# Four float32 products of a transformer block's cross stage, each written as three products of rounded parts that share tiles

## The chip, the core and the metric

The kernel runs on one core of a Trainium2 chip, in one launch. Its engines work side by side, each through a list of instructions of its own, and wait for each other by semaphores: TensorE (PE) multiplies, VectorE (DVE), ScalarE (ACT) and GpSimd (POOL) work elementwise, and SyncE (SP) here only issues DMA transfers. The metric is the device time of one execution in microseconds (us), as the median of several runs.

## What is computed

`x` is 16 blocks of 128 rows by 512 columns. Three stages follow each other, each on layer-normalised rows and added back to `x`: attention, the cross stage, and a feed-forward stage (FFN) with quantised weights. In the cross stage a block's 128 rows are the channels and its 512 columns the positions.

```python
def _L0_xattn_ref(mask, encodings, w_in, b_in, w_out, b_out, w_ct, b_ct, local_size):
    ...
    x = jnp.transpose(mask, (0, 2, 1))
    qkv = x @ w_in.T + b_in
    q, k, v = jnp.split(qkv, 3, axis=-1)
    ...
    scores = jnp.einsum('bqhd,bkhd->bhqk', q, k) / jnp.sqrt(jnp.asarray(d, q.dtype))
    ...
    scores = jnp.where(band[None, None], scores, neg)
    attn = jax.nn.softmax(scores, axis=-1)
    o = jnp.einsum('bhqk,bkhd->bqhd', attn, v).reshape(n, t, e)
    o = o @ w_out.T + b_out
    o = jnp.transpose(o, (0, 2, 1))
    y = jax.nn.relu(o) * encodings
    out = jnp.einsum('nit,io->not', y, w_ct) + b_ct[None, :, None]
```

Four of its products have a 128 x 128 weight on one side and a block of 128 x 512 on the other: the queries and the keys (`wqk`, two halves), the heads' output (`wout`), and the product behind the gate (`wct`).

## The kernel before, in words

Attention comes first. It already writes its float32 products as three products of parts: a value is rounded to the type `float32r` (high), the rest is rounded too (low), and high x high, low x high and high x low are summed in PSUM. Its lines 367 to 369 are such a product of 128 x 128 by 128 x 512. A short block of its own (`setup_cross`) then loads the cross stage's weights and makes the row scales; all engines meet at its end.

The cross stage and the FFN are one block (`cross_and_ffn`). It is written as a software pipeline by hand: each engine runs `step(b)` for b = -3 to 15, and in a step works on several blocks at once. A step on PE, ACT and DVE has eight slots (s = 0 to 7). In step b:

- PE, in every slot, first computes a unit of scores of block b+1 whose row maxima are wanted (`maximum_scores`, into PSUM tile `Sm`), then a unit of scores of block b shifted by their maxima (`shifted_scores`, into `Se`). There is one `Sm` and one `Se`: the next unit of `Sm` waits for DVE's maxima of the last one (`mx`, L1583), and the next unit of `Se` for ACT's exponentials (`x_ex`, L1262). Between the units stand the other products: probabilities times values of block b-1 in slots 0 to 2 (L1121), the heads' output of block b-2 in slot 2 (`out_product`, L1131), the values of block b+1 in slot 3 (L1162), the queries and keys of block b+3 in slots 5 and 6 (`project`, L1106), and the product behind the gate of block b-2 in slot 7 (`last_product`, L1139).
- ACT, in slot 2, copies a piece of the FFN's weights (`w_stage`, L1325, in steps 0 to 11); in slot 3 it copies the heads' sums out of PSUM (`x_oU`, L1282), in slot 4 it makes the gate's relu (`gated`, L1287), in slots 4 and 5 a logarithm and two exponentials for 1/sum (`x_rl`, L1291 and L1296), and in slots 6 and 7 the rounded queries and keys (`high`, L1273).
- DVE makes the maxima, the normalised rows of block b+3 (`normalised`, L1567, slot 4), the rests of queries and keys (`rest`, L1573, slots 6 and 7), copies and statistics.
- POOL makes the low parts of maxima, queries and keys (`maxima_low` L1404 and L1406, `low` L1410), multiplies the gate by the context (`gated`, L1415), and scales and merges the heads (`scaled` L1419, `merged` L1424).
- SP sends queries and keys out to DRAM and back into the layout of the scores (tiles `x_Q` and `x_K`), and loads weights' pieces and context.

Every engine works strictly in the order written. The last products of blocks 14 and 15 are written by hand among the first steps of the FFN. PE there has `gate_up(0, 1)`, `last_product(14)`, `rows_turned(1)`, and later `last_product(15)`, `gate_up(1, 2)`, `rows_turned(2)`; ACT has `ffn_step(0)`, `gated(15)`, `ffn_step(1)`. `rows_turned(b)` is the transpose of block b's quantised rows (L1205).

## Time and profile before

| what | value |
|---|---|
| median of the runs (3) | 1137.68 us (1136.1 to 1139.05) |
| the profiled execution's own time | 1140.24 us |
| its span on the core | 1138.4 us |
| busy: PE, DVE, ACT, POOL | 90%, 70%, 58%, 53% |
| cross stage with its fill | about 634 to 972 us of the span |
| mean granted TensorE clock | 0.964 of full speed |

The span is the profiled execution from the first instruction to the last; the difference to its own time (1.84 us) lies around it. The shares of busy time are over the whole span. A matmul record is longer than the time to the next one, since matmuls overlap in the pipeline: what one costs is read from start to start. A float32 product of 128 x 512 shows as two matmul records, one of `float32r` as one.

### The profile page before, as it was taken

The page shows a single profiled execution, that of the slowest core. Times are in us where ns is not written, and L with a number is a line of the kernel's source. Part 1 is how long each engine was busy: PE and PEld are TensorE (multiplying, and loading weights), DVE is VectorE, ACT ScalarE, POOL GpSimd, SP SyncE. Part 2 cuts the span into 40 slices and gives each one's busy share as a digit, 9 for nine tenths or more (in the row PEclk, how much of TensorE's full clock was granted, in tenths as well). Part 3 has the DMA queues.
Part 4 walks back from the last instruction along what each step waited for, and adds up shares of the span by engine and source line. Part 5 has one row for each costly group of instructions (what it writes and reads, how often), then busy time and mean ns, then how long its engine had stood idle before and what let it go on. Part 6 is the DMA issues. An engine that isn't in the chain of part 4 may idle for free. (4 is left out here: it accounts for less than half of the span.)

```text
span 1138.4 us, 25188 instructions
## 1 busy us (share of the span) xinstructions
PE 1025.3 (90%) x9588; PEld 774.2 (68%) x9604; DVE 791.7 (70%) x1444; ACT 665.1 (58%) x1204; POOL 602.7 (53%) x586
## 2 busy tenths in 40 slices
PE   6689999999999999999977378999999998789996
PEld 5578778888888888888855156666666665344443
DVE  6577867666566665666753367787878765699995
ACT  5545555545545454554653236777777666578885
POOL 3564766657567565765663523353535345455552
PEclk9899999999999999999997689999999998899999
DMA  9133543432423423323552568878787751000001
GB/s 344 54 144 153 199 174 126 148 143 81 148 96 130 148 93 130 139 100 132 173 208 93 130 149 183 176 184 176 187 180 178 157 113 56 10 20 34 33 29 37
DMA packets 51144, 147.67 MB, mean 130 GB/s; under 512 B 10448, under 2 KB 24272, under 8 KB 39760
## 3 DMA queue, kind: packets, MB, share of 16 engines
q1 hardware_dynamic: 42288, 86.93, 28.7%
q0 software_dynamic: 8064, 58.72, 14.0%
q8 instruction: 79, 1.29, 0.5%
q10 hardware_dynamic: 672, 0.40, 0.1%
q14 instruction: 41, 0.34, 0.1%
HBM read 120.46 MB, written 25.17 MB: 128 GB/s over the span
## 5 line engine op out<-in xcount | busy, mean ns | idle before, releaser
L1583 DVE TENSOR_REDUCE mx<-Sm 128x4 f32<-128x768 f32 x128 | 122.5, 957 | 78.0 <-PE Sm L1078 75.8
L282 PE MATMUL Qb<-a_xTh,WqH 128*128 128x256 f32 x512 | 147.4, 288 | 1.1 <-DVE a_vl L800 0.8
L283 PE MATMUL Qb<-a_xTl,WqH 128*128 128x256 f32 x512 | 146.6, 286 | 0.0
L284 PE MATMUL Qb<-a_xTh,WqL 128*128 128x256 f32 x512 | 146.4, 286 | 0.0
L627 POOL TENSOR_TENSOR a_pr<-a_pr_plain,a_ph 128x512 fp32r<-128x512 f32 x64 | 83.4, 1304 | 111.1 <-ACT a_ph L447 110.9
L740 DVE TENSOR_TENSOR a_turned<-Qb,sinS 64x512 f32<-64x512 f32 (+1 forms) x144 | 94.9, 659 | 65.3 <-PE Qb L284 47.8
L1262 ACT ACTIVATE x_ex<-Se 128x768 f32<-128x768 f32 x128 | 103.7, 810 | 59.8 <-PE Se L1078 59.7
L459 ACT ACTIVATE Lb<-Lb 128x512 f32<-128x512 f32 x64 | 37.2, 582 | 173.5 <-PE Ob L354 173.5
L609 POOL TENSOR_TENSOR a_ql<-a_rot,a_qh 128x512 fp32r<-128x512 f32 x64 | 84.0, 1317 | 100.1 <-ACT a_qh L467 99.9
L367 PE MATMUL Yb<-a_WoH,a_oH 128*128 128x512 f32 x256 | 103.9, 406 | 4.2 <-POOL a_oN L605 4.2
L282 PEld LDWEIGHTS Qb<-a_xTh,WqH 128*128 128x128 f32 x512 | 99.8, 195 | 4.9 <-DVE a_vl L800 1.9
L369 PE MATMUL Yb<-a_WoH,a_oN 128*128 128x512 f32 x256 | 101.9, 398 | 0.0
L368 PE MATMUL Yb<-a_WoL,a_oH 128*128 128x512 f32 x256 | 101.8, 398 | 0.0
L283 PEld LDWEIGHTS Qb<-a_xTl,WqH 128*128 128x128 f32 x512 | 99.7, 195 | 2.4
L284 PEld LDWEIGHTS Qb<-a_xTh,WqL 128*128 128x128 f32 x512 | 99.7, 195 | 0.0
L605 POOL TENSOR_TENSOR a_oN<-a_oN_plain,a_oH 128x512 fp32r<-128x512 f32 x64 | 84.4, 1319 | 4.0 <-ACT a_oH L439 4.0
L1455 POOL TENSOR_TENSOR x_hg<-x_h,x_g 128x512 f32<-128x512 f32 (+1 forms) x48 | 58.1, 1213 | 45.5 <-DVE x_h L1724 44.5
L756 DVE TRANSPOSE_TENSOR_REDUCE a_rmax<-Sb 128x16 f32<-128x512 f32 x64 | 45.6, 713 | 50.7 <-PE Sb L334 50.5
L1070 PE MATMUL Sm<-band,ident_b 128*64 128x256 bf16 x512 | 53.5, 290 | 22.7 <-DMA x_K<-k_parts 12.2
L1070 PEld LDWEIGHTS Sm<-band,ident_b 128*64 128x64 bf16 x512 | 18.4, 109 | 81.7 <-issue 43.2
L770 DVE TENSOR_TENSOR a_oN_plain<-Ob,a_rl 128x512 f32<-128x512 f32 x64 | 43.8, 684 | 42.9 <-ACT a_rl L463 42.8
L636 POOL TENSOR_TENSOR Dg<-ident,a_negm 32x512 fp32r<-32x512 f32 x64 | 66.5, 1039 | 12.9 <-DVE a_negm L763 10.0
(204 smaller groups left out, 2784.6 us busy)
## 6 DMA issues: line engine op xcount, KB each, us to landing
a_WoH<-wo_parts POOLq DMA_DIRECT2D x28, 1024.0 KB, 5.1
a_WoL<-wo_parts POOLq DMA_DIRECT2D x28, 1024.0 KB, 7.1
x_K<-k_parts SPq DMA_DIRECT2D x32, 256.0 KB, 7.5
q_parts<-x_qp SPq DMA_DIRECT2D x16, 384.0 KB, 2.8
k_parts<-x_kp SPq DMA_DIRECT2D x16, 384.0 KB, 3.5
x_Q<-q_parts SPq DMA_DIRECT2D x16, 384.0 KB, 5.5
a_w_stage<-in_gateT SPq DMA_DIRECT2D x8, 704.0 KB, 4.7
x_w_stage<-in_gateT SPq DMA_DIRECT2D x8, 704.0 KB, 5.5
```

The source lines that it names most:

```text
L282: pe.matmul(out, w_hi(k), xTh[:, k, :], start=(k == 0), stop=False)
L283: pe.matmul(out, w_hi(k), xTl[:, k, :], start=False, stop=False)
L284: mm = pe.matmul(out, w_lo(k), xTh[:, k, :], start=False, stop=(k == KD - 1))
L367: pe.matmul(Yb[s % 2][:, :], high, WoH[u % 2][:, i, :], start=(i == 0), stop=False)
L368: pe.matmul(Yb[s % 2][:, :], high, WoL[u % 2][:, i, :], start=False, stop=False)
L369: mm = pe.matmul(Yb[s % 2][:, :], low, WoH[u % 2][:, i, :], start=False, stop=(i == HG - 1))
L605: pool.tensor_tensor(oL[:, s % 2, :], oN[:, s % 2, :], oH[:, s % 2, :].bitcast(F32), ALU.subtract).then_inc(oL_ready, 1)
L609: pool.tensor_tensor(rot_dst(False, True, par, r), rbuf(par, r)[:, 0:rot_width(r)], rot_dst(True, False, par, r).bitcast(F32), ALU.subtrac ...
L627: pool.tensor_tensor(pl[:, :], pr[:, :], ph[:, :].bitcast(F32), ALU.subtract).then_inc(pl_ready, 1)
L740: dve.tensor_tensor(dst[to:to + hi - lo, 0:width].rearrange("p (j c) -> p j c", c=P), bank[lo:hi, 0:width].rearrange("p (j c) -> p j c", c=P),
L1262: act.activation(ex[:, (PAIRS * b + p) % RING, 4 * hf * WIN:4 * (hf + 1) * WIN].rearrange("p (j c) -> p j c", j=2), Se[:, :, 0:2 * WIN], A ...
L1583: dve.tensor_reduce(mx[:, half, at:at + 4].rearrange("p (j a) -> p j a", j=2), Sm[:, :, 0:2 * WIN].rearrange("p j (a c) -> p j a c", a=2), ...
```

## The change

The four products become three each, of `float32r` parts. The weights are rounded once in `setup_cross`: ACT makes the high parts, POOL the low ones, three times each. The moving sides are rounded in every step. ACT makes the high parts `x1H` (straight from `X`, by the scale and shift of the normalisation), `oH` and `yH`; POOL makes the low parts `x1L`, `oL` and `yL`. The space comes from sharing: `oH` is `x1L`'s tile, `oL` lies on the plain heads' output and `yL` on the plain gate, and the FFN weights' staging has one buffer for two. In the cross stage the rows of ones in `x_K` are written by ACT and no longer by POOL. On POOL, `merged` moves ahead of the queries' `low`. In attention and in the norms some semaphores are merged, with no instruction moved. The core of the diff:

```diff
             def project(b, half):
-                wait(pe, x1_ready, b + 1)
+                cols = slice(half * P, (half + 1) * P)
                 wait(pe, (q_rest, k_rest)[half], b)
-                return pe.matmul(XY[:, half, :], t["wqk"][:, half * P:(half + 1) * P], x1[b % 2][:, :], start=True, stop=True)
+                wait(pe, x1_high, b + 1)
+                pe.matmul(XY[:, half, :], t["wqkH"][:, cols], x1H[:, :], start=True, stop=False)
+                pe.matmul(XY[:, half, :], t["wqkL"][:, cols], x1H[:, :], start=False, stop=False)
+                wait(pe, x1_low, b + 1)
+                return pe.matmul(XY[:, half, :], t["wqkH"][:, cols], x1L[:, :], start=False, stop=True)
...
             def last_product(b):
                 wait(pe, v_ready, min(b + 4, B))
                 wait(pe, x_new, b)
-                wait(pe, y_ready, b + 1)
+                wait(pe, yH_ready, b + 1)
                 if b >= B - 2:
                     wait(pe, xqT_ready, b - B + 3)
-                pe.matmul(Ab[:, :], t["wct"][:, :], gate[:, :], start=True, stop=True).then_inc(wct_full, 1)
+                pe.matmul(Ab[:, :], t["wctH"][:, :], yH[:, :], start=True, stop=False)
+                pe.matmul(Ab[:, :], t["wctL"][:, :], yH[:, :], start=False, stop=False)
+                wait(pe, yL_ready, b + 1)
+                pe.matmul(Ab[:, :], t["wctH"][:, :], yL[:, :], start=False, stop=True).then_inc(wct_full, 1)
...
+            def rows_high(b):
+                wait(act, k_full, b)
+                act.activation(x1H[:, :], t["X"][:, b, :], ACT.Identity, scale=t["scale"][:, b:b + 1],
+                               bias=t["shift"][:, b:b + 1]).then_inc(x1_high, 1)
...
+            def heads_high(b):
+                wait(act, oN_ready, b + 1)
+                wait(act, out_full, b)
+                wait(act, k_full, min(b + 5, B))
+                act.activation(oH[:, :], oN[:, :], ACT.Copy).then_inc(oH_ready, 1)
+
+            def gate_high(b):
+                wait(act, y_ready, b + 1)
+                wait(act, wct_full, b)
+                act.activation(yH[:, :], gate[:, :], ACT.Copy).then_inc(yH_ready, 1)
...
+                    if s == 0 and real(b - 2):
+                        heads_high(b - 2)
+                    if s == 1 and real(b + 3):
+                        rows_high(b + 3)
+                    if (b, s) == (-1, 1):
+                        for i in range(len(K)):
+                            act.activation(K[i][ROWS:SHIFTED, :, :].rearrange("p h t -> p (h t)"), t["ones"][ROWS:SHIFTED, 0:1].to_broadcast([3, XH * D]),
+                                           ACT.Copy).then_inc(k_ones, 1)
                     if s == 4 and real(b - 1):
                         logarithms(b - 1)
+                    if s == 5 and real(b - 2):
+                        gate_high(b - 2)
                     if s == 5 and real(b - 1):
                         reciprocals(b - 1)
...
             for b in range(-3, B):
                 step(b)
+            heads_high(B - 2)
             rows_rounded(0)
             values_copied(B - 1)
             rows_copied(0)
             logarithms(B - 1)
             gated(B - 2)
             reciprocals(B - 1)
+            gate_high(B - 2)
             rows_rounded(1)
             act.preload_act_table(ACT.Silu)
+            heads_high(B - 1)
             ffn_step(0)
             gated(B - 1)
+            gate_high(B - 1)
             for b in range(1, B + 2):
                 ffn_step(b)
...
+            def rows_low(b):
+                wait(pool, x1_high, b + 1)
+                wait(pool, x1_ready, b + 1)
+                wait(pool, k_full, b)
+                wait(pool, out_full, b - 4)
+                pool.tensor_tensor(x1L[:, :], x1[b % 2][:, :], x1H[:, :].bitcast(F32), ALU.subtract).then_inc(x1_low, 1)
...
-                if b == -1:
-                    wait(pool, k_low, b + 3)
-                    for i in range(len(K)):
-                        wait(pool, k_ones, i)
-                        pool.memset(K[i][ROWS:SHIFTED, :, :], 1.0).then_inc(k_ones, 1)
-                    wait(pool, k_ones, len(K))
+                if real(b - 2):
+                    heads_low(b - 2)
                 if real(b - 2):
                     gated(b - 2)
                 if real(b + 1):
                     maxima_low(b + 1, 0)
+                if real(b + 3):
+                    rows_low(b + 3)
+                if real(b - 2):
+                    gate_low(b - 2)
                 if real(b - 1):
                     scaled(b - 1)
+                    merged(b - 1)
                 if real(b + 3):
                     low(qp, qr, b + 3, q_mid, q_low)
-                if real(b - 1):
-                    merged(b - 1)
```

`out_product` changes as `last_product` does (`woutH` and `woutL`, `oH` and `oL`); `heads_low` and `gate_low` are subtractions like `rows_low`.

ACT in slots 4 to 7 of a full step of the kernel before, after the gate's relu and up to the keys' rounding:

```order
L1287 ACTIVATE x_gate<-Bb,bo 128x512
L1268 ACTIVATE x_m<-Bb 32x64
L1262 ACTIVATE x_ex<-Se 128x768
L1291 ACTIVATE x_rl<-x_rl 128x1024
L1262 ACTIVATE x_ex<-Se 128x768
L1296 ACTIVATE x_rl<-x_rl,live 128x512 x2
L1273 ACTIVATE x_qp<-XY,bqk 128x512
L1262 ACTIVATE x_ex<-Se 128x768
L1273 ACTIVATE x_kp<-XY,bqk 128x512
```

And the same place of the changed kernel, where `x_yL_plain` is the gate:

```order
L1314 ACTIVATE x_yL_plain<-Bb,bo 128x512
L1290 ACTIVATE x_m<-Bb 32x64
L1284 ACTIVATE x_ex<-Se 128x768
L1329 ACTIVATE x_rl<-x_rl 128x1024
L1284 ACTIVATE x_ex<-Se 128x768
L1325 ACTIVATE x_yH<-x_yL_plain 128x512
L1334 ACTIVATE x_rl<-x_rl,live 128x512 x2
L1300 ACTIVATE x_qp<-XY,bqk 128x512
L1284 ACTIVATE x_ex<-Se 128x768
L1300 ACTIVATE x_kp<-XY,bqk 128x512
```

The gate's rounding (L1325) stands between the exponentials of slot 5 and everything that ACT does in slots 6 and 7. The other two new instructions stand in slots 0 and 1.

POOL in a full step of the kernel before, from the keys' low part on:

```order
L1410 TENSOR_TENSOR x_kp<-x_kr,x_kp 128x512
L1415 TENSOR_TENSOR x_gate<-x_gate,x_ctxb 128x512
L1404 TENSOR_TENSOR x_m<-x_mr,ones 32x64
L1406 TENSOR_TENSOR x_m<-x_mr,x_m 32x64
L1419 TENSOR_TENSOR x_oU<-x_oU,x_rl 128x1024
L1410 TENSOR_TENSOR x_qp<-x_qr,x_qp 128x512
L1424 TENSOR_TENSOR x_oN<-x_oU 128x512
```

And the same step of the changed kernel (`x_oL_plain` is the heads' output, `x_x1L` the low part of the rows):

```order
L1470 TENSOR_TENSOR x_kp<-x_kr,x_kp 128x512
L1484 TENSOR_TENSOR x_oL<-x_oL_plain,x_x1L 128x512
L1475 TENSOR_TENSOR x_yL_plain<-x_yL_plain,x_ctxb 128x512
L1457 TENSOR_TENSOR x_m<-x_mr,ones 32x64
L1459 TENSOR_TENSOR x_m<-x_mr,x_m 32x64
L1466 TENSOR_TENSOR x_x1L<-x_x,x_x1H 128x512
L1489 TENSOR_TENSOR x_yL<-x_yL_plain,x_yH 128x512
L1479 TENSOR_TENSOR x_oU<-x_oU,x_rl 128x1024
L1494 TENSOR_TENSOR x_oL_plain<-x_oU 128x512
L1470 TENSOR_TENSOR x_qp<-x_qr,x_qp 128x512
```

Three subtractions are new. The rows' one (L1466) stands behind the gate's product with the context and both halves of `maxima_low`.

ACT where the cross stage gives way to the FFN, in the changed kernel, from the end of `ffn_step(0)` into `ffn_step(1)`:

```order
L1393 ACTIVATE x_sq,x_ss<-x_h 128x512
L1314 ACTIVATE x_yL_plain<-Bb,bo 128x512
L1325 ACTIVATE x_yH<-x_yL_plain 128x512
L1393 ACTIVATE x_sq,x_ss<-x_h 128x384
L1385 ACTIVATE x_silu<-Se,x_f 128x512
```

The rounding L1325 is new between the gate's relu (L1314) and block 0's last squares (L1393, in the kernel before L1344).

## Rows read from the trace of the kernel before

**Rows 1.** Windows, cross stage: busy us of PE, PEld, DVE, ACT, POOL; clock, DMA share, GB/s.

```profile
634.00:661.00 27.00, 11.55 (x56) 5.54 (x56) 7.12 (x8) 5.49 (x9) 15.22 (x7) 0.63 0.75 159
...
800.00:880.00 80.00, 79.23 (x1469) 54.70 (x1473) 64.38 (x107) 57.84 (x85) 38.29 (x40) 1.00 0.79 183
```

**Rows 2.** Timeline of PE: start us, duration us, what; two starts of step, and attention.

```profile
565.34 0.39 PE L367 MATMUL Yb<-a_WoH,a_oH 128*128 128x512 f32 x1
565.57 0.39 PE L368 MATMUL Yb<-a_WoL,a_oH 128*128 128x512 f32 x1
...
839.94 0.41 PE L1070 MATMUL Sm<-band,ident_b 128*64 128x256 bf16 x4
...
857.79 1.13 PE L1139 MATMUL Ab<-x_gate,wct 128*128 128x512 f32 x2
858.85 0.41 PE L1070 MATMUL Sm<-band,ident_b 128*64 128x256 bf16 x4
```

**Rows 3.** Timeline of ACT in slots 4 to 6 of the step that starts at 839.94.

```profile
849.86 0.70 ACT L1287 ACTIVATE x_gate<-Bb,bo 128x512 f32<-128x512 f32 x1
...
851.83 0.81 ACT L1262 ACTIVATE x_ex<-Se 128x768 f32<-128x768 f32 x1 [0.44 <-PE Se L1078]
...
853.48 0.80 ACT L1262 ACTIVATE x_ex<-Se 128x768 f32<-128x768 f32 x1
854.17 1.33 ACT L1296 ACTIVATE x_rl<-x_rl,live 128x512 f32<-128x512 f32 x2
855.39 0.69 ACT L1273 ACTIVATE x_qp<-XY,bqk 128x512 bf16<-128x512 f32 x1
```

**Rows 4.** Timeline of DVE in slots 6 and 7 of the same step.

```profile
855.15 0.96 DVE L1583 TENSOR_REDUCE mx<-Sm 128x4 f32<-128x768 f32 x1
856.11 0.75 DVE L1573 SCALAR_TENSOR_TENSOR x_qr<-XY,bqk,x_qp 128x512 f32<-128x512 f32 x1
...
857.38 0.95 DVE L1583 TENSOR_REDUCE mx<-Sm 128x4 f32<-128x768 f32 x1
```

**Rows 5.** Timeline of POOL, and PE's queries product, in the same step.

```profile
850.63 1.27 POOL L1415 TENSOR_TENSOR x_gate<-x_gate,x_ctxb 128x512 f32<-128x512 f32 x1 [6.39 <-ACT x_gate L1287]
852.00 0.55 POOL L1404 TENSOR_TENSOR x_m<-x_mr,ones 32x64 bf16<-32x64 f32 x1
852.63 0.29 POOL L1406 TENSOR_TENSOR x_m<-x_mr,x_m 32x64 bf16<-32x64 f32 x1
...
853.34 1.12 PE L1106 MATMUL XY<-x_x,wqk 128*128 128x512 f32 x2
```

**Rows 6.** One instruction's cost, by groups (mean ns of one): a rounding and its rest.

```profile
L439 ACT ACTIVATE a_oH<-a_oN_plain 128x512 fp32r<-128x512 f32 x7 | 4.4, 631 | 3.0 <-DVE a_oN_plain L770 3.0
L605 POOL TENSOR_TENSOR a_oN<-a_oN_plain,a_oH 128x512 fp32r<-128x512 f32 x8 | 10.2, 1280 | 4.0 <-ACT a_oH L439 4.0
```

**Rows 7.** Timeline of ACT where the cross stage fills.

```profile
633.17 1.28 ACT L1255 ACT_TABLE_LOAD   x1 [3.31 <-PEq L903]
635.92 0.69 ACT L1273 ACTIVATE x_qp<-XY,bqk 128x512 bf16<-128x512 f32 x1 [1.47 <-PE XY L1106]
...
664.64 0.21 ACT L1268 ACTIVATE x_m<-Bb 32x64 bf16<-32x64 f32 x1 [18.78 <-PE Bb L1101]
```

**Rows 8.** Timeline of ACT, DVE, POOL and PE where the cross stage gives way to the FFN.

```profile
980.75 0.69 ACT L1336 ACTIVATE x_silu<-Sm,x_f 128x512 f32<-128x512 f32 x1
...
990.14 0.52 ACT L1344 ACTIVATE x_sq<-x_h 128x384 f32<-128x384 f32 x1
...
992.80 0.74 DVE L1724 SCALAR_TENSOR_TENSOR x_h<-Se,x_f,x_silu 128x512 f32<-128x512 f32 x1
...
981.34 1.32 POOL L1424 TENSOR_TENSOR x_oN<-x_oU 128x512 f32<-128x512 f32 x1
...
991.15 1.71 POOL L1415 TENSOR_TENSOR x_gate<-x_gate,x_ctxb 128x512 f32<-128x512 f32 x1
...
998.67 0.59 PE L1205 MATMUL T<-ident_b,x_xq 128*128 128x128 bf16 x4 [3.16 <-DVE X L1621]
```

More of the change, by code:

```diff
@@ L919, in _ @@
             act.activation(t["band"][:, :], band[:, :], ACT.Copy)
+            act.wait_ge(w_in, 16 * len(names))
+            for name in ("wqk", "wout", "wct"):
+                act.activation(t[name + "H"][:, :], plain[name][:, :], ACT.Copy).then_inc(weights_high, 1)
         @block.sync
@@ L985, in cross_and_ffn @@
             h, sq = sb("h", [P, F], F32, later), sb("sq", [P, 512], F32, later)
-        w_stage = [sb(f"w_stage{i}", [P, WIDEST], F32) for i in range(2)]
+        w_stage = sb("w_stage", [P, WIDEST], F32)
         Q, K = [sb("Q0", [P, XH, D], BF16)], [sb("K0", [P, XH, D], BF16)]
@@ L1003, in cross_and_ffn @@
         x1 = [sb(f"x1{i}", [P, D], F32) for i in range(2)]
+        x1H, x1L = sb("x1H", [P, D], F32R), sb("x1L", [P, D], F32R)
+        oH = x1L
         Vw, mx = t["Vw"], t["mx"]
@@ L1334, in silu_chunk @@
                     wait(act, w_whole, len(PIECES))
+                    wait(act, se_full, SLOTS * B)
                 wait(act, h_ready, n - 1)
@@ L1419, in scaled, with heads_low, gate_low @@
                 pool.tensor_tensor(oU[:, :, :], oU[:, :, :], rl[:, :, :], ALU.mult).then_inc(oU_scaled, 1)
+            def heads_low(b):
+                wait(pool, oH_ready, b + 1)
+                wait(pool, out_full, b)
+                pool.tensor_tensor(oL[:, :], oN[:, :], oH[:, :].bitcast(F32), ALU.subtract).then_inc(oL_ready, 1)
+            def gate_low(b):
+                wait(pool, yH_ready, b + 1)
+                wait(pool, wct_full, b)
+                pool.tensor_tensor(yL[:, :], gate[:, :], yH[:, :].bitcast(F32), ALU.subtract).then_inc(yL_ready, 1)
             def merged(b):
@@ L1497, in _ @@
             maxima_low(B - 1, 1)
+            heads_low(B - 3)
             variance_root(1, "r1", 0, FIRST)
-            variance_root(2, "r2", 0, FIRST)
+            variance_root(4, "r2", 0, FIRST)
             gated(B - 3)
+            gate_low(B - 3)
             scaled(B - 2)
             merged(B - 2)
+            heads_low(B - 2)
             row_factor(0)
             gated(B - 2)
+            gate_low(B - 2)
             scaled(B - 1)
             merged(B - 1)
+            heads_low(B - 1)
             row_factor(1)
@@ L1543, in step @@
                 if 0 <= b + 1 < len(PIECES):
-                    wait(sp, w_whole, b)
-                    load_piece(sp, dram, b + 1, w_stage[(b + 1) % 2]).then_inc(w_in[(b + 1) % 2], 16)
+                    wait(sp, w_whole, b + 1)
+                    load_piece(sp, dram, b + 1, w_stage).then_inc(w_in, 16)
                 if real(b + 3):
@@ L1604, in offset @@
                 i, lo, hi = PIECES[n]
-                piece = w_stage[n % 2][:, 0:hi - lo]
-                wait(dve, w_in[n % 2], 16 * (n // 2 + 1))
+                piece = w_stage[:, 0:hi - lo]
+                wait(dve, w_in, 16 * (n + 1))
                 dve.tensor_scalar(piece, piece, t["w_inv"][:, i:i + 1], MAGIC, ALU.mult, ALU.add).then_inc(w_rounded, 1)
@@ L1666, in variances @@
                 wait(dve, x1_ready, B)
+                wait(dve, x1_high, B)
                 for b in range(lo, hi):
@@ L1701, in rows_scale @@
                 wait(dve, f1_ready, b)
-                wait(dve, n_scaled, 1 if b < FIRST else 2)
+                wait(dve, n_step, 5 if b < FIRST else 10)
                 dve.tensor_scalar(bound[:, :], amax[:, :], scale, EPS, ALU.mult, ALU.max).then_inc(bound_ready, 1)
```

105 lines of the change are left out of this document (61 added, 44 removed).

## The prediction

> **What bounds the kernel now.** I read the windows of the cross stage first. Of the 80 us between 800 and 880 us PE is busy for 79.23, at the full clock (1.00, which is 2.4 GHz); DVE is busy for 64.38, ACT for 57.84 and POOL for 38.29 [rows 1]. PE sets the pace there. The reader is to see two things beside that: ACT has about 22 us of 80 left, and the DMA engines are at 0.79.
>
> Next the timeline. A full step starts at 839.94 and the next one at 858.85 [rows 2]: 18.91 us. Shares say nothing on how the work lies within a step, so I looked at each engine from slot to slot. In slots 4 to 7 the picture differs. ACT begins the exponentials of slot 4 at 851.83 and from there on has no wait: slot 5's exponentials at 853.48, the two exponentials of `x_rl` at 854.17, the queries' rounding at 855.39 [rows 3]. That rounding ends at 855.39 + 0.69 = 856.08, and DVE's rest of the queries starts at 856.11, right behind it. DVE then goes on without a wait to the last maxima of the step, at 857.38 to 858.33 [rows 4]. PE's next step can't start before these maxima, since its first unit writes `Sm`. It starts at 858.85: with some 0.05 us for the signal, the chain ACT, DVE, `Sm` has 0.47 us to spare in a step. This small number decides what the change is worth.
>
> **The change part by part, a full step.** A float32 product costs 858.85 - 857.79 = 1.06 us from start to start. A `float32r` product of the same size costs 565.57 - 565.34 = 0.23 us [rows 2], so three cost 0.69. That saves 0.37 us a product and 4 x 0.37 = 1.48 us of PE in a step, which would give a step of 17.43 us if PE alone set it.
>
> ACT gains three roundings of 0.63 us and POOL three subtractions of 1.28 us, as the same operations on tiles of this size take in attention [rows 6]. From start to start I take 0.59 for the rounding, as neighbours on ACT overlap by some 0.04. By the sums this fits: ACT 57.84 / 80 x 18.91 = 13.7 us, and 15.5 with them; POOL 9.1 and 12.9.
>
> By place: `heads_high` (slot 0) and `rows_high` (slot 1) fall where ACT waits for `Se`, and I cost them at nothing; without that cover each would cost up to its 0.59. `gate_high` stands in slot 5, in front of the `x_rl` exponentials and the queries' rounding, in the full stretch. So the chain moves by two terms. Up to slot 4 PE sets the time, and only one product has become shorter (the heads' output in slot 2): -0.37. In slot 5 ACT has 0.59 more: +0.59. The queries' rounding, DVE's rest, and the last maxima come 0.22 later in the step. They end at 858.33 - 839.94 + 0.22 = 18.61, and the next step starts at 18.61 + 0.05 = 18.66. A full step gets shorter by 0.25 us and not by 1.48; PE waits for the rest, before slot 0's first unit.
>
> A second chain ends at nearly the same place: the rows' low part, for which PE waits in the middle of the queries' product. The gate's relu starts at 849.86, which is set by ACT's work in slots 2 and 3 and doesn't move. POOL's product with the context ends at 851.90, `maxima_low` at 852.92 [rows 3, 5]; then `rows_low` takes 1.28, to 854.2 or, with the small gaps between POOL's instructions, 854.3. The queries' product was at 853.34 [rows 5] and would now start at some 852.95 and have its two high parts done at 853.4. So PE stalls 0.9 us, starts the last part at 854.35 and slot 6 at 854.6, 0.2 later than now. Slot 6's maxima on DVE may come up to 0.25 later (they start at 855.15 now, and the queries' rounding ends only 0.22 later than now) before they in turn delay the chain above. So this wait is just hidden, and it is the first thing to break the forecast: whatever makes POOL 0.1 later lengthens the step.
>
> On the lock between the two engines there is a row: `maxima_low`'s first half takes 0.55 us here, beside the normalisation on DVE at 851.9, though its second half, of the same size, takes 0.29 [rows 5]. The Trainium skill, "SBUF — State Buffer", section "Who interferes with whom", says why such pairs shut each other out: they share a pair of ports as an exclusive lock for the whole instruction. By that rule the added 3.84 us of POOL a step speak against the change: a DVE instruction of that kind may wait for a whole subtraction; the row agrees, and the case is in the second rival.
>
> POOL's other two subtractions have room: `heads_low` follows the keys' low part and is done over 1 us before slot 2's last part wants it; `gate_low` has two slots. The queries' `low`, put behind `merged`, leaves 1.3 us later; its transfer is wanted in the next step only. The single `w_stage` is freed in slot 2 and filled from slot 4 on, 11 us ahead of its use. SP gets no new transfers in the loop. All nothing.
>
> There are eleven steps with four products (2 to 12): 11 x -0.25 = -2.8. Steps 13 to 15 have two products and the same `gate_high` in ACT's full stretch; I take nothing there (+0 to -1). Steps 0 and 1 lack the gate and heads' products; nothing.
>
> **The fill.** ACT's table load ends at 633.17 + 1.28 = 634.45, and the queries' rounding of block 0 starts at 635.92 [rows 7]. Now `rows_high` (0.69, as the rounding with a bias [rows 3]) and `rows_low` (1.28) come between, and then the last part of the product, twice 0.23 since the clock there is mostly half (0.63 in the mean) [rows 1], with 0.16 of drain: 634.45 + 0.69 + 1.28 + 0.46 + 0.16 = 637.04, which is +1.1. The weights' parts before it (three small pairs on ACT and POOL, behind the last weights' arrival) end some 0.35 later than the block does now. The transfers of block 0's keys follow and nothing else runs beside them, so it goes through: +1.5. Block 2's queries wait for POOL in the same way, +0.3. The ones in `x_K` (4096 elements a row, three times) are on ACT at most eight times a rounding of 512 each, 3 x 8 x 0.63 = 15.1 us, within ACT's idle 18.78 us [rows 6, 7]: nothing. Sum +1.8.
>
> **The way into the FFN.** Two new roundings stand on ACT in front of FFN work and wait for POOL. `heads_high(15)` waits for `merged(15)`, which now stands behind `gate_low(14)`: 981.34 + 1.32 = 982.66 plus 1.3 is 984.0. So the first silu starts at about 984.65, not 980.75 [rows 8]; its tile was read by DVE only at 984.52, so 3.9 us become +0.85. Then `gate_high(15)` waits for POOL's product with the context, which ends at 991.15 + 1.71 = 992.86 [rows 8], now + 0.85: 993.7. The last squares of block 0 stood at 990.14 and now start at 994.35. DVE's mean square and the `x_h` behind it, at 992.80 now, need the squares (0.7 us) and the silu behind them (0.7): 995.8, or +3.0. From there to the transpose of block 2 at 998.67 both engines follow each other with no gap over 0.4, and DVE goes on full into the FFN. +3.0 goes through. It takes in the 0.85.
>
> **Sum.** -2.8 + 1.8 + 3.0 = +2.0 us. The profiled execution's own 1140.24 (span 1138.4) becomes 1142.2. The median of the runs is 1137.68, 2.6 below the profiled one, so I predict 1139.7 us.
>
> **The rivals.**
> - *PE's saving goes through* (0.1). For it: PE has 79.23 of 80. Against it: the 0.47 us of [rows 3, 4]. Eleven steps of 17.43 are -16.3; with +4.8 at the ends the time is 1126. A half-way house, where ACT's start in slot 4 comes forward more than I see, gives -0.6 a step and 1136 (0.15, inside "no change" for the most part).
> - *POOL lengthens the step* (0.27): the rows' low part comes 0.4 us later than I have it, by the port lock or by the longer list on POOL. It decides from 0.1 us on. At 0.4 later slot 6 starts 0.6 later than now, the maxima 0.4 beyond what is hidden, and a full step is 18.66 + 0.4 = 19.06: 11 x +0.15 = +1.7 instead of -2.8, so +6.5 and 1144. For it: the doubled `maxima_low`; against it: POOL's stretches are otherwise steady.
> - *The ends cost less* (0.13): the squares find cover, or the fill's transfers hide the later start; +1 for +4.8, so 1136.
> - My forecast (0.35) itself, 1137 to 1142.
>
> **How the numbers follow.** A measurement tells a change from none at about 0.3%, 3.4 us: 1134.3 to 1141.1. Faster takes in the first rival and a little of the half-way house and the third: 0.18. Slower takes in the second rival and the upper quarter of my own case: 0.36. No change 0.46. The range holds all but the first rival and the ends: 1131 to 1146.
>
> **What would show it.** Right: fp32r products 0.23 apart; PE's wait for POOL before the last part of the queries' product, some 0.9 us a step; a PE wait for `mx` at each step's start; a step of 18.6 to 18.7; ACT full from slot 4 to 7; the transpose of block 2 some 3 us later against the last values' product. Wrong: a step under 18.2 with PE free of waits, or one over 18.9 with the `x1L` wait over 1.3 us; x_K's ones on ACT beyond its idle time.

## The result and the profile after

The changed kernel takes 1147.85 us (median of 5 runs, 1145.22 to 1150.87). The kernel before took 1139.05 us beside it (5 runs, 1136.1 to 1142.77). The ratio is 1.0077, 95% interval 1.0057 to 1.0097: slower by 8.8 us. I had predicted 1139.7, no change, range 1131 to 1146.

The profiled execution has a span of 1148.2 us against 1138.4. The table cuts both at the same instructions: the first product with a cross weight (`bv_out`, 631.17 and 629.82), ACT's `x_m` of slot 4 of step -1 (664.64 [rows 7] and 666.16), `x_m` of slot 0 of later steps, and the transpose of block 2 (998.67 [rows 8] and 1008.24). A "typical step" is the median of steps 2 to 12.

| stretch, us | before | after | difference | predicted |
|---|---|---|---|---|
| attention, up to `bv_out` | 631.2 | 629.8 | -1.35 | 0 |
| fill, to slot 4 of step -1 | 33.47 | 36.34 | +2.87 | +1.8 |
| rest of step -1 | 7.83 | 10.47 | +2.64 | 0 |
| steps 0 and 1 | 36.06 | 36.12 | +0.06 | 0 |
| steps 2 to 12 | 208.14 | 209.36 | +1.22 | -2.8 |
| of which the typical step | 18.91 | 18.89 | -0.02 | -0.25 |
| steps 13 and 14 | 35.40 | 36.14 | +0.74 | 0 |
| step 15 to block 2's transpose | 46.60 | 49.99 | +3.39 | +3.0 |
| rest of the FFN | 139.76 | 139.91 | +0.15 | 0 |

Windows of the changed kernel, in the columns of [rows 1]:

```profile
634.00:661.00 27.00, 10.24 (x48) 5.90 (x48) 7.01 (x8) 17.39 (x14) 7.21 (x6) 0.50 0.70 151
664.00:668.00 4.00, 3.51 (x31) 2.40 (x31) 2.37 (x6) 0.21 (x1) 1.17 (x3) 0.50 0.32 68
672.00:680.00 8.00, 6.85 (x68) 5.02 (x68) 4.47 (x7) 2.83 (x6) 2.56 (x4) 0.50 0.32 120
800.00:880.00 80.00, 77.80 (x1443) 57.24 (x1439) 67.96 (x107) 65.33 (x98) 52.17 (x52) 1.00 0.81 182
```

The same windows of the kernel before, where no row stood:

```profile
664.00:668.00 4.00, 2.74 (x32) 1.48 (x30) 3.63 (x7) 0.90 (x2) 0.78 (x2) 1.00 0.01 1
672.00:680.00 8.00, 6.55 (x108) 5.21 (x107) 5.44 (x6) 5.24 (x7) 1.78 (x4) 1.00 0.56 154
```

Two things stand out. From 664 to 680 us the granted clock, last but two in a row, is 0.50 where it was 1.00: TensorE runs at 1.2 GHz and not 2.4. PE is busy for 6.85 of 8 us with 68 matmul records, where it was 6.55 with 108. And in the full steps PE has become less busy (77.80 of 80, from 79.23 [rows 1]) though its work is shorter: it now waits.

The timeline of PE in the full step that starts at 864.30 (the same step as in [rows 2], one later):

```profile
864.30 0.41 PE L1082 MATMUL Sm<-band,ident_b 128*64 128x256 bf16 x4
...
871.14 0.50 PE L1147 MATMUL Bb<-x_x1L,woutH 128*128 128x512 f32 x1
...
871.48 0.40 PE L1148 MATMUL Bb<-x_x1L,woutL 128*128 128x512 f32 x1
...
871.72 0.40 PE L1150 MATMUL Bb<-x_oL,woutH 128*128 128x512 f32 x1
...
872.04 0.41 PE L1082 MATMUL Sm<-band,ident_b 128*64 128x256 bf16 x4
...
878.43 0.19 PEld L1122 LDWEIGHTS XY<-x_x1L,wqkH 128*128 128x128 f32 x1 [0.56 <-POOL x_x1L L1466]
...
878.87 0.41 PE L1082 MATMUL Sm<-band,ident_b 128*64 128x256 bf16 x4
...
883.23 0.41 PE L1082 MATMUL Sm<-band,ident_b 128*64 128x256 bf16 x4
```

A product in parts takes 872.04 - 871.14 = 0.90 us. The parts lie 0.34 and 0.24 apart, and 0.32 pass from the last to the next kind of matmul. The 0.23 of [rows 2] is right for a neighbour of the same kind; another 0.21 goes to the two ends of the group, where the kind of matmul changes. That it is the change of kind, and not something else at the ends, was not tried by itself.

ACT, DVE and POOL in slots 5 to 7 of this step, which answer to [rows 3 to 5]:

```profile
877.11 1.27 POOL L1466 TENSOR_TENSOR x_x1L<-x_x,x_x1H 128x512 fp32r<-128x512 f32 x1
...
877.73 0.80 ACT L1284 ACTIVATE x_ex<-Se 128x768 f32<-128x768 f32 x1
...
878.42 0.63 ACT L1325 ACTIVATE x_yH<-x_yL_plain 128x512 fp32r<-128x512 f32 x1
...
878.94 1.33 ACT L1334 ACTIVATE x_rl<-x_rl,live 128x512 f32<-128x512 f32 x2
...
880.16 0.68 ACT L1300 ACTIVATE x_qp<-XY,bqk 128x512 bf16<-128x512 f32 x1
...
880.88 0.75 DVE L1650 SCALAR_TENSOR_TENSOR x_qr<-XY,bqk,x_qp 128x512 f32<-128x512 f32 x1 [0.29 <-ACT x_qp L1300]
...
882.14 0.94 DVE L1660 TENSOR_REDUCE mx<-Sm 128x4 f32<-128x768 f32 x1
```

The chain that I described is there. The queries' rounding starts 15.86 us into the step (15.45 before [rows 2, 3]), DVE's rest waits for it, and the last maxima end at 883.08, 0.15 ahead of the next step. The waits from 720 to 930 us (us in total, times, longest) say what is new. The three below `mx` were not in the trace of before; for `mx` PE's weight load waited longer there, 20.3 us:

```profile
PEld Sm L1082 <- DVE mx L1660: 7.1, 22, 0.4
...
PEld XY L1122 <- POOL x_x1L L1466: 6.4, 11, 0.6
...
DVE x_qr L1650 <- ACT x_qp L1300: 3.0, 11, 0.3
...
PE Sm L1082 <- DMA x_K<-k_parts: 0.8, 2, 0.5
```

The fill, which answers to [rows 7]:

```profile
629.82 0.58 PE L933 MATMUL bv_out<-bv,wout_plain 128*128 128x1 f32 x2 [7.85 <-DMA live<-in_live]
...
632.21 1.28 ACT L1277 ACT_TABLE_LOAD   x1 [1.59 <-PEq L902]
...
633.50 0.81 ACT L1294 ACTIVATE x_x1H<-X,shift,scale 128x512 fp32r<-128x512 f32 x1
...
634.39 1.27 POOL L1466 TENSOR_TENSOR x_x1L<-x_x,x_x1H 128x512 fp32r<-128x512 f32 x1 [2.48 <-ACT x_x1H L1294]
...
636.55 0.69 ACT L1300 ACTIVATE x_qp<-XY,bqk 128x512 bf16<-128x512 f32 x1 [2.24 <-PE XY L1122]
...
647.82 10.62 ACT L1362 ACTIVATE x_K<-ones 3x4096 bf16<-3x4096 f32 x3
...
666.16 0.21 ACT L1290 ACTIVATE x_m<-Bb 32x64 bf16<-32x64 f32 x1 [7.72 <-PE Bb L1113]
```

The ones in `x_K` take ACT 10.62 us and are hidden. The queries' rounding comes 6.73 us after `bv_out`; it was 635.92 - 631.17 = 4.75.

The way into the FFN, which answers to [rows 8]:

```profile
987.24 2.83 DVE L1770 SCALAR_TENSOR_TENSOR x_xg<-X,mv,x_g 128x512 f32<-128x512 f32 x1
...
991.23 0.63 ACT L1320 ACTIVATE x_x1L<-x_oL_plain 128x512 fp32r<-128x512 f32 x1 [3.63 <-POOL x_oL_plain L1494]
991.76 0.67 ACT L1385 ACTIVATE x_silu<-Sm,x_f 128x512 f32<-128x512 f32 x1
...
1000.86 0.63 ACT L1325 ACTIVATE x_yH<-x_yL_plain 128x512 fp32r<-128x512 f32 x1 [2.77 <-POOL x_yL_plain L1475]
1001.40 0.51 ACT L1393 ACTIVATE x_sq<-x_h 128x384 f32<-128x384 f32 x1
...
1008.24 0.59 PE L1227 MATMUL T<-ident_b,x_xq 128*128 128x128 bf16 x4 [1.29 <-DVE X L1698]
```

Both roundings hold ACT while they wait for POOL (3.63 and 2.77 us), each ahead of FFN work, as predicted.

### The profile page after: what moved, and what is told of

Its sections match the earlier page's. It is cut to its first block and busy times, and to the rows that moved or that the text cites. A ratio compares the mean times of both kernels' runs of the same rounds, so it can differ in the third digit from the quotient of the medians.

```text
span 1148.2 us, 25520 instructions
## 1 busy us (share of the span) xinstructions
PE 1028.1 (90%) x9651; PEld 789.0 (69%) x9668; DVE 802.8 (70%) x1444; ACT 702.2 (61%) x1258; POOL 653.8 (57%) x634
## 5 line engine op out<-in xcount | busy, mean ns | idle before, releaser
L635 POOL TENSOR_TENSOR Dg<-ident,a_negm 32x512 fp32r<-32x512 f32 x64 | 66.5, 1039 | 13.3 <-DVE a_negm L762 10.5
L466 ACT ACTIVATE a_qh<-a_rot 128x512 fp32r<-128x512 f32 x64 | 40.4, 632 | 46.1 <-DVE a_rot L750 45.7
```

## The experiments

Most kernels use one switch: the lists `PROJ`, `OUT` and `GATE` name the blocks whose product is in parts, and any other block takes a float32 product, without roundings and low parts. Where `GATE` is empty, its weight `wct` isn't rounded either; the other two, `wqk` and `wout`, are rounded in every run. The unchanged kernel before ran beside each of them.

**1. The gate in float32** (`gate_fp32`).

```diff
+PROJ, OUT, GATE = list(range(B)), list(range(B)), list(())
...
+                if b not in GATE:
+                    wait(pe, y_ready, b + 1)
+                    pe.matmul(Ab[:, :], t["wct"][:, :], gate[:, :], start=True, stop=True).then_inc(wct_full, 1)
+                    return
```

> The product behind the gate stays float32 (no rounding of the gate on ACT or POOL), the other three stay in parts. Theory 1 (the step is set by two chains, ACT's full stretch with the gate's rounding in it, and the rows' low part on POOL): ACT's chain is freed, the POOL chain stays, so the full step goes from 18.9 to about 18.85 only (slot 6 still starts at 14.57 into the step, then 2.07 and 2.23), and the way into the FFN gets about 2.5 us back: 3 us under the changed kernel. Rival (the gate's rounding alone takes the gain): the step falls to 18.4, and with the end it is 8 us under.

Measured: 1142.35 us (ten executions, one of them at 1973.43; 1142.18 without it), ratio 1.0014 (1.0003 to 1.0026). The typical step is 18.89, as in the changed kernel; the tail from step 15 on is 45.01 (49.99), the fill with the rest of step -1 35.61 and 9.25 (36.34 and 10.47). So taking the gate out of parts wins 5.5 us on the changed kernel's median, more than the 3 expected, and most of it in the tail (5.0), not in the step: there its rounding and its saving on PE go away together.

**2. The gate's rounding shrunk** (`gate_col`): 16 of 512 columns after block 0, so that the other columns keep block 0's high part.

```diff
-                act.activation(yH[:, :], gate[:, :], ACT.Copy).then_inc(yH_ready, 1)
+                n = D if b == 0 else 16
+                act.activation(yH[:, 0:n], gate[:, 0:n], ACT.Copy).then_inc(yH_ready, 1)
```

> The gate's rounding on ACT covers 16 of 512 columns for all blocks but the first (the rest of the output is wrong there); all else stays. Theory 1: ACT has some 0.4 us less in slot 5, but the rows' low part still holds slot 6, so PE's own work from there gives a step of 18.7, 0.2 less, and 2 to 3 us in all. Rival (gate's rounding alone): the step falls by the whole 0.4 us, to 18.5, and 5 us in all. If the step stays at 18.9, PE's products and neither chain set it.

Measured: 1143.79 us, ratio 1.0037 (1.0017 to 1.0058). The typical step is 18.69. DVE's wait for the queries' rounding is gone in ten of eleven steps (0.3 us in all, 3.0 in the changed kernel), and PE's for the rows' low part is unchanged:

```profile
PEld XY L1122 <- POOL x_x1L L1467: 6.4, 11, 0.6
...
DVE x_qr L1651 <- ACT x_qp L1300: 0.3, 1, 0.3
```

So the rounding costs 18.89 - 18.69 = 0.20 us a step. It doesn't account for all that the step lacks. The tail is 48.22 here.

**3. The last two roundings behind FFN work** (`tail_order`).

```diff
+                if b == 0:
+                    heads_high(B - 1)
+                if b == 1:
+                    gate_high(B - 1)
...
-            heads_high(B - 1)
             ffn_step(0)
             gated(B - 1)
-            gate_high(B - 1)
```

> Only the order of ACT at the way into the FFN: block 15's heads are rounded behind the first silu, and its gate behind the first silu of block 1, no longer ahead of block 0's last squares. Theory: most of the 3.4 us lost there comes back, 2 to 3 us under the changed kernel. Rival (PE's or POOL's added work makes the loss): under 0.7 us.

Measured: 1145.7 us, ratio 1.0052 (1.0035 to 1.0068). The tail is 47.20 (49.99), the steps as in the changed kernel (19.04 in the mean). Of the 3.4 us that the tail lost, 2.8 are the place of these two instructions together.

**4. Float32 at both ends** (`ends_fp32`): queries and keys of blocks 0 to 2, heads and gate of blocks 14 and 15, from the high parts of the weights (their low parts are left out there).

```diff
+PROJ, OUT, GATE = list(range(3, B)), list(range(B - 2)), list(range(B - 2))
```

> Blocks 0 to 2 have float32 queries and keys, and blocks 14 and 15 float32 output and gate products (on the high part of the weights alone, the low part is left out there); the eleven full steps stay as changed, apart from one or two blocks. Theory: the fill gets its start back, the clock rises at about 664 us as before and not at 681, and the way into the FFN too: 6 to 8 us under the changed kernel, so about the time of before. Rival (the full steps make the loss): 2 us under.

Measured: 1143.29 us, ratio 1.0021 (1.0004 to 1.0038). Typical step 18.89 and tail 45.94; the fill 34.83 and 8.73, with the clock rising at 670.3 us and not 680.6. That is 4.6 us under the changed kernel, short of the 6 to 8 expected, and still above the kernel before.

**5. The rows' low part earlier** (`early`): experiment 1 with a third buffer for the normalised rows, so that DVE normalises in slot 2 and POOL subtracts ahead of the gate.

```diff
-        x1 = [sb(f"x1{i}", [P, D], F32) for i in range(2)]
+        x1 = [sb(f"x1{i}", [P, D], F32) for i in range(3)]
...
+                if real(b + 3):
+                    rows_low(b + 3)
                 if real(b - 2):
                     gated(b - 2)
...
+                    if s == 2 and real(b + 3) and real(b + 1):
+                        normalised(b + 3)
```

> As gate_fp32 (the gate product stays float32), and the plain rows have a third buffer, so that DVE normalises block b+3 in slot 2 and POOL makes its low part ahead of the gate, not behind it. Theory 1: with both chains out of the way PE alone sets the full step; its three products are each 0.16 shorter than in float32, so 18.91 - 0.48 = 18.43 to 18.5; with the fill still 2 us late it ends 2 to 3 us under the kernel before. If the step stays at 18.85 or more, the POOL chain wasn't what held it (then DVE's full stretch or the transfers).

Measured: 1138.21 us, ratio 0.9999 (0.9985 to 1.0014). PE in a full step of it:

```profile
839.91 0.41 PE L1091 MATMUL Sm<-band,ident_b 128*64 128x256 bf16 x4
...
854.09 0.41 PE L1091 MATMUL Sm<-band,ident_b 128*64 128x256 bf16 x4
...
858.39 0.41 PE L1091 MATMUL Sm<-band,ident_b 128*64 128x256 bf16 x4
```

That is 18.48, which is also the typical step (five of the eleven take 18.44), against 18.89 in experiment 1, and PE no longer waits for `x_x1L`. Slot 6 starts 14.18 us into the step and not 14.57. So this wait, 0.6 us long, cost 18.89 - 18.48 = 0.41 us a step. With it gone, three products in parts give 18.91 - 18.48 = 0.43 us of 3 x 0.16 = 0.48: nearly all that PE saves arrives. The edit moves DVE's normalisation out of slot 4 as well, so the two were not told apart here; but in experiment 8 the normalisation stays in slot 4, there is no such wait, and PE's saving arrives too. The median is 0.7 us under the kernel before, where 2 to 3 were expected: the fill is late here as well (35.37 and 8.26).

**6. PE kept busy in the fill** (`fill_busy`): 18 products whose output nobody reads, in step -1.

```diff
+                    if b == -1 and s < 3:
+                        for _ in range(6):
+                            pe.matmul(Ab[:, 0:2 * P], t["woutH"][:, :], t["wqkH"][:, :], start=True, stop=True)
```

> The changed kernel, with 18 products of constants (128 x 256) added on PE in the first three slots of the fill's last step, where PE waits for DVE anyway; nothing reads them. Theory: in the fill PE has too little to do after its new waits, and the clock stays at half until 681 us; with more work it rises by 670 us, the second half of that step takes 8 us and not 10.5, and the kernel ends 2 to 3 us earlier than the changed one. Rival (the late rise is only where it happened to fall): no change in the rise, or 1 to 2 us more time for the added work.

Measured: 1145.43 us, ratio 1.006 (1.0041 to 1.0079). The windows:

```profile
661.00:671.00 10.00, 8.32 (x78) 5.67 (x78) 6.79 (x12) 1.46 (x3) 2.07 (x3) 0.84 0.47 102
671.00:681.00 10.00, 7.41 (x120) 5.78 (x118) 7.05 (x8) 6.58 (x10) 2.92 (x4) 0.99 0.47 141
681.00:695.00 14.00, 12.08 (x194) 8.47 (x192) 8.40 (x14) 6.86 (x11) 5.00 (x7) 0.88 0.81 172
```

The clock rose early, at 660.9 us, but was at half again from 667.8 to 671.2 and from 691.6 to 695.1. The fill and the rest of step -1 got shorter (35.17 and 9.47), steps 0 and 1 longer by 1.4 (37.55): 0.7 us in all by the profile. The median is 2.4 under the changed kernel's, of four executions, and the intervals of the two ratios overlap, so a gain isn't shown. What the trace does point to is that the clock follows PE's own work: in the four profiles with the same fill but without the added products it rose at 674.5 to 681.5. (In `gate_fp32`, with one weight's rounding less, it was 666.3, so single profiles scatter widely.)

**7. Six parts for one product** (`six_parts`): three more parts in the heads' product, which changes what is computed there.

```diff
-                pe.matmul(Bb[:, :], t["woutH"][:, :], oL[:, :], start=False, stop=True).then_inc(out_full, 1)
+                pe.matmul(Bb[:, :], t["woutH"][:, :], oL[:, :], start=False, stop=False)
+                pe.matmul(Bb[:, :], t["woutL"][:, :], oL[:, :], start=False, stop=False)
+                pe.matmul(Bb[:, :], t["woutL"][:, :], oL[:, :], start=False, stop=False)
+                pe.matmul(Bb[:, :], t["woutL"][:, :], oL[:, :], start=False, stop=True).then_inc(out_full, 1)
```

> The heads' output product has six parts and not three (the output is off by the added ones). If a product of parts is three times 0.23 plus about 0.2 us for the change of shape before and behind it, the six take 0.9 + 0.69 = 1.6 us from start to start. If each part costs 0.30, they take 1.8.

Measured: 1157.74 us (one execution). PE:

```profile
855.28 0.50 PE L1147 MATMUL Bb<-x_x1L,woutH 128*128 128x512 f32 x1
855.61 0.40 PE L1148 MATMUL Bb<-x_x1L,woutL 128*128 128x512 f32 x1
...
856.55 0.39 PE L1153 MATMUL Bb<-x_oL,woutL 128*128 128x512 f32 x1
856.87 0.41 PE L1082 MATMUL Sm<-band,ident_b 128*64 128x256 bf16 x4
```

Six parts take 1.59 us, three 0.90: 0.23 a part and 0.2 for the surroundings. The typical step is 19.59, longer by 0.70, or 3 x 0.23. What PE has to do in slot 2 goes through into the step in full. The fill, whose instructions are the changed kernel's, took 36.30 and 9.73 here, with the clock up at 674.5.

**8. The heads' output alone in parts** (`out_only`), the other three float32: `PROJ` and `GATE` are empty.

> Only the heads' output product is in parts; queries, keys and gate stay float32. Its rounding on ACT lies in slot 0 and its rest on POOL in a gap of 5 us. Theory 1: the full step is 18.91 - 0.16 = 18.75, nothing is late in the fill, and only the rounding of block 15's heads delays the first silu (+0.9): 1 to 2 us under the kernel before. Rival (a product in parts gains nothing on PE by itself): the time of before or 1 us over it.

Measured: 1136.02 us, ratio 0.998 (0.996 to 1.0): 2.9 us under the kernel before, where 1 to 2 were expected, and just at the edge of the interval. Typical step 18.79 (-0.12; four of the eleven take 18.75); the fill 33.58 and 7.83 with the clock up at 661.6, and the tail 45.13.

**9. Only the first three blocks' queries and keys in float32** (`fill_fp32`): `PROJ = list(range(3, B))`, the rest as changed.

> The changed kernel, but the queries' and keys' products of blocks 0 to 2 alone are float32 again (one product each, from the block as VectorE leaves it and the high part of the weights, so the low parts of these are left out of the computation), and the parts x1H and x1L of blocks 0 to 2 are not made; from block 3 on nothing differs from the changed kernel, and the roundings of the weights stay. Theory A: the 5.5 us that the changed kernel loses before step 0 are the parts of the first blocks, about half as work of the fill and about half as TensorE's clock, which stayed at half speed 16.7 us longer. Then the fill takes about 33.5 to 34.5 us, the clock rises at about 662 to 670, the rest of step -1 takes about 8 us, steps 2 to 12 keep about 19.0 us each and the tail about 49 to 50 us: some 4 to 5 us under the changed kernel, 1143 to 1144. Rival B: the clock is late because of the weights' roundings, or by chance; then the clock rises at about 680 all the same, the fill saves 2 to 3 us and the median is about 1145.5. Rival C: what is saved ahead of step 0 is given back in steps 0 and 1, under 1 us in all.

Measured: 1145.68 us, ratio 1.0049 (1.0032 to 1.0067). The fill is 34.57 and the rest of step -1 8.62, together 3.6 us shorter than in the changed kernel; the clock rises at 669.3. Steps and tail are as there (18.99, 49.17). The first theory holds for the trace; the saving in the median, 2.2 us, is smaller than the 4 to 5 that it said.

**10. Queries and keys alone in parts** (`proj_only`): `OUT` and `GATE` are empty.

> The changed kernel with only the queries' and keys' products in parts; the heads' output and the gate are float32 products again, their parts and roundings gone. Theory A (the product in parts of queries or keys gives PE little, 1.06 us against 0.90 for three products with the changes of shape around them, and lies beside other work): the fill and the clock are late as in the changed kernel (about 36 and 10 us, rise near 680), the step stays at about 18.9 to 19.0 us, and the tail goes back to about 45 to 46 us; the median is about 1142. Rival B: the projections alone carry what the full step loses, since GpSimd has the low part of x1; then the step is 19.05 or more. Rival C: the step falls to 18.6, since nothing of the gate's is left on ScalarE, and the median is about 1138.

Measured: 1143.48 us, ratio 1.0036 (1.0017 to 1.0055). The fill is late as in the changed kernel (35.60 and 10.46, clock up at 681.3), the tail 44.96. The typical step is 19.02, longer than before the change:

```profile
PEld XY L1131 <- POOL x_x1L L1487: 6.6, 11, 0.6
...
PE XY L1131 <- POOL x_x1L L1487: 1.7, 11, 0.2
```

That is next to rival B's 19.05 (the mean of steps 2 to 12 is 19.05), and not the fall to 18.6 of rival C: the wait for the rows' low part costs more than two products save. The median is 1.5 us over theory A's 1142.

**11. What these point to, together** (`best`): gate in float32, heads in parts, queries and keys in parts from block 3 on with experiment 5's early low part, the last heads' rounding behind the first silu.

```diff
+PROJ, OUT, GATE = list(range(3, B)), list(range(B)), list(())
```

> What the earlier runs point to, together: the gate in float32; the heads' output in parts in every block; the queries and keys in float32 for blocks 0 to 2 and in parts from block 3 on, with the low part of x1 on GpSimd ahead of the gate's work and the block normalised one slot earlier into a third buffer; the last heads' rounding behind the first silu. Theory A (each place at which the parts cost something is kept in float32, each place where they shorten the chain is kept in parts): fill and clock as before (33.5 and 7.8 us, rise near 662), steps 2 to 12 at about 18.5 to 18.65 us, tail about 45 us, median 1132 to 1135, 4 to 6 us under the kernel before. Rival B: the third buffer and the float32 weights beside the rounded ones add nothing, but the step is set by the transfers of the keys' parts in some steps, so that it stays at 18.8, and the median is about 1136, as with the heads' output alone. Rival C: the step's gain is eaten by steps 0 and 1, where the clock falls again; median 1137 to 1139.

Measured: 1137.11 us, ratio 0.9975 (0.9959 to 0.999): faster than the kernel before, by 2.8 us, and not by the 4 to 6 expected. The typical step is 18.48, the mean of steps 2 to 12 18.55, the tail 45.23, as expected. The fill wasn't: 34.42 and 8.71, with the clock up at 668.0. Its gain is no larger than that of the heads' output alone (experiment 8, 2.9 us).

```profile
800.00:880.00 80.00, 79.23 (x1576) 58.66 (x1578) 69.48 (x106) 63.38 (x95) 48.05 (x50) 1.00 0.79 180
```

PE is back at 79.23 of 80 us, with 1576 matmul records, where the kernel before had 1469 [rows 1].

## Why the prediction was wrong

**The step.** The prediction had "three cost 0.69. That saves 0.37 us a product". This is the term that was mis-sized first: a product in parts costs 0.90, so it saves 1.06 - 0.90 = 0.16. The two ends' 0.21 are in the 1.06, which was read up to the next matmul of another kind, and not in the 0.23. With 0.16 for 0.37 the prediction's own sum for a step would be 18.66 + 0.21 = 18.87, next to the measured 18.89. That would have been right by luck: if ACT's chain alone had bound, experiment 1 would have brought the step down to PE's own 18.91 - 0.48 = 18.43, and it stayed at 18.89.

The second failure is a step of the argument: that PE sets the time only up to slot 4, and that the wait for the rows' low part is "just hidden". The typical steps show instead that PE's time and this wait go into the step nearly in full. Three prices give them all within 0.05 us: -0.16 for a product in parts (1.06 less 0.90), +0.41 for the wait wherever queries and keys are in parts with the late subtraction (experiments 1 and 5), and +0.20 for the gate's rounding where its product is in parts too (experiment 2).

| kernel | sum | typical step by it | measured |
|---|---|---|---|
| changed | -0.64 + 0.41 + 0.20 | 18.88 | 18.89 |
| `gate_col` | -0.64 + 0.41 | 18.68 | 18.69 |
| `gate_fp32` | -0.48 + 0.41 | 18.84 | 18.89 |
| `proj_only` | -0.32 + 0.41 | 19.00 | 19.02 |
| `out_only` | -0.16 | 18.75 | 18.79 |
| `early`, `best` | -0.48 | 18.43 | 18.48 |

No price comes from `proj_only` and `out_only`, so these rows test them. The prediction had the times in this place nearly right: the subtraction ends 14.08 us into the step, where 14.36 was forecast, and PE's slot 6 starts at 14.57 (14.66). What it had wrong is what that costs: work that PE does later in slots 6 and 7 isn't caught up before the step ends. The start of slot 6 in the kernel before, in the step of [rows 2], is

```profile
854.39 0.41 PE L1070 MATMUL Sm<-band,ident_b 128*64 128x256 bf16 x4
```

From there to the next step PE takes 858.85 - 854.39 = 4.46 us, and in `early`, where one of the two products behind it is in parts, 858.39 - 854.09 = 4.30: the 0.16 arrives in full, and PE has no slack in these two slots either. In the changed kernel it is 883.23 - 878.87 = 4.36, close to 4.46 - 2 x 0.16 and the 0.20 of the gate's rounding. The chain through ACT, which I had bind alone, only adds its 0.20 on top. So of the second rival the mechanism was right (the wait for the rows' low part lengthens the step), its cause was not (POOL late by the port lock). And the first rival was right in that PE's time goes through, with 0.16 and not 0.37 a product to give.

**Two disturbed steps.** The mean of the changed kernel's steps is 19.03, its typical one 18.89: two steps take 19.84 and 19.51. PE's two waits for `x_K`, 0.8 us in all, lie in these two, and so does one of 0.6 for `x_Q`; together they are most of the 1.57 us by which the two exceed the typical step. Before, none of these steps exceeded 18.99, and PE waited for no transfer. I had costed the transfers at nothing. In `early` and `best` there are such waits too, of 0.2 to 0.7 us each; what makes the transfers late was not tried.

**The fill.** The prediction had +1.8; the fill took +2.87, and the rest of step -1 another +2.64 that I had at nothing. The work part was right in kind: the rounding with a bias takes 0.81 (0.69 forecast), the queries' rounding comes 1.98 later, not 1.5. What is missing in the prediction is the clock. In the kernel before, TensorE is granted the full clock in pieces during the fill (0.63 in the mean [rows 1]) and without a break from 664.0 us to the FFN. In the changed kernel it stays at half from 626.0 to 680.6. The same late rise, at 680.9 to 681.5, is in `gate_col`, `tail_order` and `proj_only`. With float32 for blocks 0 to 2 it comes at 669.3, 670.3 and 668.0, and with all queries and keys in float32 at 661.6. The rest of step -1 follows it: 10.46 to 10.47 in the four late kernels, 9.73 in `six_parts`, 8.62 to 8.73 in the middle, 7.83 in `out_only`. Over many executions the changed kernel has less of the full clock too: the mean granted clock over 29 executions of the kernel before is 0.965, over the changed kernel's five 0.953, over `best`'s twelve 0.964. As the clock is either full or half, the time at half is twice what is missing: 2 x 0.035 x 1138 = 80 us before, 2 x 0.047 x 1146 = 107 us after. These means don't say where it is missing. In the two profiles, 14 of the 24 us more at half lie ahead of 700 us and 10 behind 960 us, on the way into the FFN.

Why is only partly shown. In the fill PE waits for transfers and other engines, and the parts leave it with less to do: 10.24 us busy of 27 against 11.55 [rows 1], at a lower clock. The Trainium skill, "TensorE: Matmul & The Clock Gate", section "HAM oscillation — how this bites in real kernels", says that an engine left waiting for transfers falls back to the slow clock and starts its next work there. The trace agrees in kind (0.70 to 0.75 DMA share and a clock of 0.50 to 0.63 in the fill), but PE's wait for `x_K`, the longest there, is 9.4 us now and 9.5 before, so it isn't what tells the two kernels apart. That more work on PE brings the rise forward is what `fill_busy` points to.

The instructions alone do not fix the moment. `six_parts` has those of the changed kernel up to step 0, and its clock rose at 674.5, 6 us earlier. `gate_fp32` and `proj_only` have the same ones as each other (all queries and keys in parts, one weight's rounding less), and the clock rose at 666.3 in the first, with two falls of 3.4 us until 697.1, and at 681.3 in the second. Their windows, `six_parts` first, then `gate_fp32` and `proj_only`:

```profile
672.00:676.00 4.00, 2.85 (x24) 1.77 (x25) 2.88 (x4) 1.20 (x2) 1.15 (x1) 0.69 0.47 169
...
664.00:668.00 4.00, 3.51 (x34) 2.39 (x32) 2.13 (x5) 0.21 (x1) 0.90 (x3) 0.71 0.29 64
...
680.00:684.00 4.00, 3.62 (x54) 3.06 (x53) 3.06 (x3) 3.66 (x5) 0.41 (x1) 0.84 0.46 130
```

So part of the +2.64 is the scatter of single executions, and each of these profiles is only one; which of PE's waits decides the moment stays open. So does the third of the loss before step 0 that `fill_fp32` leaves: 1.9 of 5.5 us.

**The way into the FFN.** The number was right, +3.4 for +3.0, with the two instructions named, but part of that is luck. Experiment 3 gives 2.8 of it back by moving them. In every kernel with the whole gate in float32 the tail is shorter than before the change: 44.96 in `proj_only`, where the heads aren't rounded either, and 45.01 to 45.23 in `gate_fp32`, `early`, `out_only` and `best`, where they are (46.60 before). So the heads' rounding costs 0.3 us there at most by itself; the 5.0 us hang on the gate's parts. Its rounding on ACT is some of it (`gate_col` gives 1.8 back); its low part on POOL, behind which the heads' merge has to wait, was not tried alone. Something else in the change gives 1.6 back, which the prediction did not have. All these kernels keep `merged` ahead of the queries' low part; that it is this order was not tried alone. Nor was the clock: it is at half for 27.2 us between 967 and 1012 us in the changed kernel, for 17.0 before (961 to 1002 us), and for 13.6 in `gate_fp32`, `out_only` and `proj_only`, and no run shows whether that is a cause or follows from PE's waits.

**Steps 13 to 15.** Costed at 0 to -1; steps 13 and 14 took +0.74. In `gate_col` they take 35.32 against 36.14, `gate_fp32` 35.08: it is the gate's rounding on ACT.

**The sum.** Against its own +2.0 the span moved by +9.8. Steps 2 to 12 account for 4.0 of the error, the fill and step -1 for 3.7, the rest for little; attention, in which no instruction moved, gave 1.35 the other way.

## What to carry to other kernels

Price a replaced operation with its neighbours: from the start of the last instruction before it to the start of the first behind it, for the old and the new form alike. Here the change of matmul kind ate more than half of the saving. Before a wait is called hidden, ask whether the waiting engine has free time left in the loop; PE had 0.8 us in 80 idle, so its 0.6 us went through, and moving the subtraction ahead was worth more than twice what a product in parts saves. And where a pipeline fills, follow the clock of TensorE through it, in more than one profile: here the rest of step -1 took 7.8 to 10.5 us as the clock rose at 661.6 to 681.5, and the same instructions gave different moments.

## What the runs showed of the hardware

The float32r product of 128 x 512 costs 0.23 to 0.24 us next to its like and 0.2 us more once for a group between matmuls of another kind, whether the group has three parts (0.90 us) or six (1.59 us).

DVE's scaling of 128 x 1536 elements took 2.07 us beside POOL's heads' subtraction; the same instruction took 1.01 at 844.23 in the trace of before:

```profile
868.57 1.29 POOL L1484 TENSOR_TENSOR x_oL<-x_oL_plain,x_x1L 128x512 fp32r<-128x512 f32 x1
868.60 2.07 DVE L1684 TENSOR_SCALAR x_w_stage<-x_w_stage,w_inv 128x1536 f32<-128x1536 f32 x1
```

It is 1.06 us longer; 1.26 us of POOL's instruction were left when it started. By the rule cited ahead of the result (the Trainium skill, "SBUF — State Buffer", "Who interferes with whom") the shared ports are locked for a whole instruction, and the trace agrees to within 0.2 us. It cost nothing: the maxima behind it ended at 871.53, and PE's next unit of `Sm` started at 872.04.
